# Deformable stage on TensorE: samples in column groups by tap, and one more tile of lead for the corner weights

## What is computed

```python
offset = conv2d(x, offset_w, offset_b)          # 3x3, 18 maps
mask = sigmoid(conv2d(x, mask_w, mask_b))       # 3x3, 9 maps
py = hs + ky + dy; px = ws + kx + dx            # one sampling point for each pixel and tap
val = gather(y0, x0) * w00 + gather(y0, x0 + 1) * w01 + gather(y0 + 1, x0) * w10 + gather(y0 + 1, x0 + 1) * w11
out = einsum('bkhwc,bkhw,ock->bohw', val, mask, w_r)     # 9 taps, 32 -> 32 channels
x = x + out                                     # x is normalised before the block
```

## Time and profile before

| | us |
|---|---|
| median of 3 runs | 2346.87 |
| lowest and highest | 2318.73, 2351.54 |
| the profiled execution | 2314.87 |
| its span in the profile | 2313.1 |
| attention, to | 850.17 |
| deformable stage, near part | 850.17 to 1573.10 |
| of this steady, from spread(2) to the last samples | 922.51 to 1564.84 |
| the rest | 1573.10 to 2313.10 |

### The profile page before, as it was taken

How to read it: one execution, slowest core, us unless ns; L and a number is a source line. 1 busy time by engine, 2 the same in 40 slices (tenths; PEclk the granted TensorE clock), 3 DMA queues, 4 the chain that set the end, 5 groups by cost and what they waited for, 6 DMA issues and landing times. The chain is left out here.

```text
span 2313.1 us, 46229 instructions
## 1 busy us (share of the span) xinstructions
PE 2045.3 (88%) x14981; PEld 1256.5 (54%) x14981; DVE 1281.6 (55%) x2688; ACT 1133.4 (49%) x3617; POOL 788.5 (34%) x743
## 2 busy tenths in 40 slices
PE   5699999999999963999999999995694999999999
PEld 3566666666666641232333333324682877777776
DVE  5178888888888871555555555555336222222222
ACT  2378888888888853555555555540121111111111
POOL 0178788787887841222222222210000110110110
PEclk9889999999999985898898998887777999999999
DMA  4300000000000015444444444415002112112110
GB/s 165 110 25 27 26 24 27 26 28 26 26 27 26 24 45 144 123 133 127 121 126 120 123 133 129 108 47 91 10 10 66 34 34 66 33 33 65 34 33 14
DMA packets 169883, 149.70 MB, mean 65 GB/s; under 512 B 60645, under 2 KB 159563, under 8 KB 169694
## 3 DMA queue, kind: packets, MB, share of 16 engines
q1 hardware_dynamic: 169774, 148.38, 24.2%
HBM read 83.68 MB, written 45.89 MB: 56 GB/s over the span
## 5 line engine op out<-in xcount | busy, mean ns | idle before, releaser
L412 ACT ACTIVATE at_probs<-at_sc,at_nmx 128x196 f32<-128x196 f32 x1152 | 473.7, 424 | 116.9 <-DVE at_nmx L358 114.8
L340 POOL TENSOR_TENSOR at_probs<-at_probs,at_rs 128x784 f32<-128x784 f32 x288 | 429.9, 1493 | 156.6 <-DVE at_rs L363 156.6
L447 PE MATMUL at_pt<-at_ident,at_probs 128*98 128x128 f32 x2304 | 312.7, 279 | 40.7 <-DVE at_pts L368 40.1
L358 DVE TENSOR_REDUCE at_nmx<-at_sc 128x4 f32<-128x784 f32 x288 | 277.7, 964 | 124.7 <-PE at_sc L436 124.7
L1237 ACT ACTIVATE dn_mix<-dn_mps 128x432 f32<-128x432 f32 x384 | 182.6, 527 | 297.3 <-PE dn_mps L1139 296.8
L447 PEld LDWEIGHTS at_pt<-at_ident,at_probs 128*98 128x98 f32 x2304 | 242.0, 129 | 142.2 <-POOL at_probs L340 78.6
L436 PE MATMUL at_sc<-at_kw,at_qw 32*128 32x196 f32 x2304 | 273.5, 357 | 12.0 <-POOL at_qw L329 8.0
L1330 DVE COPY dn_sampled<-dn_sps 128x432 f32<-128x432 f32 x192 | 116.7, 608 | 252.3 <-PE dn_sps L1150 251.4
L1139 PE MATMUL dn_mps<-dn_stack,dn_selw 42*128 42x432 f16 x768 | 199.0, 383 | 52.9 <-DMA dn_stack<-near_corners 47.4
L1323 DVE TENSOR_SCALAR dn_mix<-dn_mps 128x432 f32<-128x432 f32 x384 | 213.8, 598 | 44.4 <-PE dn_mps L1139 44.4
L2014 PE MATMUL fc_qps<-fc_wk,fc_xs 99*128 99x128 f32 x1728 | 207.9, 277 | 31.6 <-DMA fc_xs<-in_ones 31.6
(11 more groups left out here) (153 smaller groups left out, 2397.6 us busy)
## 6 DMA issues: line engine op xcount, KB each, us to landing
fc_xs<-fc_xp SPq DMA_DIRECT2D x144, 120.0 KB
dn_slab<-near_image SPq DMA_DIRECT2D x72, 200.0 KB, 3.7
at_vs<-attention_values SPq DMA_DIRECT2D x288, 49.0 KB
near_corners<-dn_split SPq DMA_DIRECT2D x24, 486.0 KB
dn_stack<-near_corners SPq DMA_DIRECT2D x24, 486.0 KB
dn_patch<-near_pixels SPq DMA_DIRECT2D x24, 384.0 KB
attention_values<-ap_vrow SPq DMA_DIRECT2D x21, 256.0 KB, 2.3
near_image<-dn_chunk SPq DMA_DIRECT2D x24, 200.0 KB, 1.9
```

The costliest lines, as they stand in the source:

```text
L340: nc.gpsimd.tensor_tensor(probs[s][p][:, :, :, :], probs[s][p][:, :, :, :], rs[s][:, 2 * p:2 * p + 2, :].unsqueeze(3).broadcast_to([P, 2, ...
L358: nc.vector.tensor_reduce(nmx[s][:, 2 * p:2 * p + 2, :], sc[p][:, :, 0:2 * NK].rearrange("p b (j k) -> p b j k", j=2), AX.X, ALU.max, nega ...
L412: nc.scalar.activation(probs[s][p][:, b, j, :], sc[p][:, b, NK * j:NK * j + NK], ACT.Exp, bias=nmx[s][:, 2 * p + b, j:j + 1], accum_out=su ...
L447: mm = nc.tensor.transpose(pt[b % 2][0:HK, o:o + P], probs[s][p][:, b % 2, j, HK * c:HK * c + HK], ident[:, :])
```

## The change

*Samples.* Taps 0 to 7 are now laid out by column group: tap 4u + g of batch b goes to columns 32g of the array, and to columns 96b + 48u of sps. Each batch has four matmuls of 2 x 48 = 96 columns, and tap 8 one of 48 in the batch's old place: 20 matmuls a step in place of 4. So sampled has four taps on its partitions, and one contraction matmul of 128 rows sums over four taps and 32 channels: contract is three calls of four matmuls, for each batch into its 32 columns, at k = 1 to 3. wd shrinks to six 128 x 32 blocks.

*Lead.* Maps, hats and corner weights run one tile further ahead: conv(t + 4), bias_maps(t + 3), prepare(t + 2) at k = 1 to 4, high(t + 2) at k = 6, with the calls ahead of the loops added to match, among them conv(3) ahead of spread(0). SyncE's list is reordered, with store_corners(t + 1) first.

*Maps.* The maps are stored by batch and tap, y, x and mask next to each other, and one transfer loads all three, each row three times. residual moves from k = 6 to 4, and stack has batch ahead of tap.

```diff
-        stack = [sb(f"stack{i}", [STACK, TAPS, B, 3 * DR, THIRD], F16) for i in range(2)]
+        stack = [sb(f"stack{i}", [STACK, B, TAPS, 3 * DR, THIRD], F16) for i in range(2)]
...
-                for a, to in enumerate((hat_y, off_x, mask)):
-                    sp.dma_start(to[:, :], map_d[j % 2, TAPS * a:TAPS * a + TAPS, :, :].rearrange("k b n -> (k b) n").unsqueeze(1).broadcast_to([TAPS * B, 3, DPX])
-                                 ).then_inc(rep_in, 16)
+                sp.dma_start(offs[:, :, :].rearrange("p a n -> p (a n)"),
+                             map_d[j % 2, :, :, :].rearrange("b (k a) n -> (b k) (a n)", a=3).unsqueeze(1).broadcast_to([B * TAPS, 3, 3 * DPX])).then_inc(rep_in, 16)
...
             load_slab(2)
+            load_maps(1)
             store_corners(0)
             load_stack(0)
-            load_maps(1)
             store_pixels(2)
             store_image(4)
             store_pixels(3)
+            store_maps(2)
+            load_slab(3)
+            load_maps(2)
+            store_image(5)
             for t in range(DTILES):
                 if t + 1 < DTILES:
+                    store_corners(t + 1)
                     load_patch(t + 1)
-                save(t)
-                if t + 2 < DTILES:
-                    store_maps(t + 2)
                 if t + 3 < DTILES:
-                    load_slab(t + 3)
+                    store_maps(t + 3)
+                if t + 4 < DTILES:
+                    load_slab(t + 4)
+                if t + 1 < DTILES:
+                    load_stack(t + 1)
                 if t + 4 < DTILES:
                     store_pixels(t + 4)
-                if t + 5 < DTILES:
-                    store_image(t + 5)
-                if t + 2 < DTILES:
-                    load_maps(t + 2)
-                if t + 1 < DTILES:
-                    store_corners(t + 1)
-                    load_stack(t + 1)
+                if t + 6 < DTILES:
+                    store_image(t + 6)
+                save(t)
+                if t + 3 < DTILES:
+                    load_maps(t + 3)
...
                 for b in range(B):
-                    mm = nc.tensor.matmul(sps[C * b:C * b + C, 0:COLS], patch[t % 2][:, k, C * b:C * b + C], mix[s % 2][b][:, :], start=True, stop=True)
+                    fours = mix[s % 2][b][:, 0:8 * PX].rearrange("p (u g n) -> p u g n", u=2, g=4)
+                    for g in range(4):
+                        nc.tensor.matmul(sps[C * g:C * g + C, 2 * PX * b:2 * PX * b + 2 * PX], patch[t % 2][:, k, C * b:C * b + C], fours[:, :, g, :], start=True, stop=True)
+                for b in range(B):
+                    mm = nc.tensor.matmul(sps[C * b:C * b + C, 8 * PX:COLS], patch[t % 2][:, k, C * b:C * b + C], mix[s % 2][b][:, 8 * PX:COLS], start=True, stop=True)
...
-                mm = nc.tensor.matmul(ops[:, 0:DPX], wd[:, k, :], sampled[t % 2][:, k, :, :].rearrange("p m i -> p (m i)"), start=(k == 0), stop=(k == TAPS - 1))
-                if k == TAPS - 1:
+                for b in range(B):
+                    w, n = (k, 2 * b + k) if k < 2 else (2 + b, 8)
+                    mm = nc.tensor.matmul(ops[C * b:C * b + C, 0:DPX], wd[:, w, :], sampled[t % 2][:, n, :, :].rearrange("p m i -> p (m i)"),
+                                          start=(k == 0), stop=(k == 2))
+                if k == 2:
...
             for kx in range(3):
                 conv(2, kx)
+            for kx in range(3):
+                conv(3, kx)
             spread(0)
...
-                    if t >= 1:
-                        for tap in range(2 * k - 2, 2 * k):
-                            if 0 <= tap < TAPS:
-                                contract(t - 1, tap)
-                    if t + 3 < DTILES and k >= 5:
-                        conv(t + 3, k - 5)
+                    if t >= 1 and 1 <= k < 4:
+                        contract(t - 1, k - 1)
+                    if t + 4 < DTILES and k >= 5:
+                        conv(t + 4, k - 5)
...
-                    if t + 2 < DTILES and k == 0:
-                        bias_maps(t + 2)
-                    if t + 1 < DTILES and k == 2:
-                        high(t + 1)
-                    if t + 2 < DTILES and k >= 4:
-                        prepare(t + 2, k - 4)
+                    if t + 3 < DTILES and k == 0:
+                        bias_maps(t + 3)
+                    if t + 2 < DTILES and 1 <= k < 5:
+                        prepare(t + 2, k - 1)
+                    if t + 2 < DTILES and k == 6:
+                        high(t + 2)
```

More of the change, by code:

```diff
@@ L869 @@
 THIRD = W // 3
-COLS = TAPS * DR * DBW
+PX = DR * DBW
+COLS = TAPS * PX
 PATCH = (DR + 4) * (DBW + 4)
@@ L953, in stage_deform_near @@
                            (wd[:, :, :], dcn), (ident[:, :], ident_d),
-                           *((stack[i][DATA:STACK, :, :, :, :].rearrange("p t b m i -> p (t b m i)"), bars) for i in range(2))))
+                           *((stack[i][DATA:STACK, :, :, :, :].rearrange("p b t m i -> p (b t m i)"), bars) for i in range(2))))
         mean, rstd = agg[:, 0:1], agg[:, 3:4]
@@ L961, in stage_deform_near @@
         patch = [sb(f"patch{i}", [PATCH, DSTEPS, P]) for i in range(2)]
-        hat_y = sb("hat_y", [NROWS, DPX])
-        off_x = sb("off_x", [NROWS, DPX])
-        mask = sb("mask", [NROWS, DPX])
+        offs = sb("offs", [NROWS, 3, DPX])
+        hat_y, off_x, mask = (offs[:, a, :] for a in range(3))
         hat_x = sb("hat_x", [NROWS, 3, DPX])
@@ L1036, in store_maps @@
                 for b in range(B):
-                    sp.dma_start(map_d[j % 2, :, b, :], maps[j % 2][C * b:C * b + 27, :, :].rearrange("p m i -> p (m i)")).then_inc(map_out, 16)
+                    sp.dma_start(map_d[j % 2, b, :, :], maps[j % 2][C * b:C * b + 27, :, :].rearrange("p m i -> p (m i)")).then_inc(map_out, 16)
             def load_maps(j):
@@ L1056, in load_stack @@
                     sp.wait_ge(mix_done, B * DSTEPS * (j - 1))
-                sp.dma_start(stack[j % 2][0:DATA, :, :, :, :].rearrange("p t b m i -> p (t b) (m i)"),
+                sp.dma_start(stack[j % 2][0:DATA, :, :, :, :].rearrange("p b t m i -> p (b t) (m i)"),
                              corner_d[j % 2, :, :].rearrange("(g r) (h n) -> (r h) g n", r=3, n=DPX)).then_inc(stack_in, 16)
@@ L1138, in spread @@
                             pe.wait_ge(mix_act, 2 * (s - 1) + b - 1)
-                    nc.tensor.matmul(mps[b][:, 0:COLS], selw[:, :], stack[t % 2][:, :, b, :, 4 * k:4 * k + 4], start=True, stop=True).then_inc(mix_done, 1)
+                    nc.tensor.matmul(mps[b][:, 0:COLS], selw[:, :], stack[t % 2][:, b, :, :, 4 * k:4 * k + 4], start=True, stop=True).then_inc(mix_done, 1)
             def sample(s):
@@ L1202, in distance_y @@
             def distance_y(j):
-                act.wait_ge(rep_in, 48 * (j + 1))
-                rows = hat_y[:, :].rearrange("p (r n) -> p r n", r=DR)
+                act.wait_ge(rep_in, 16 * (j + 1))
+                rows = hat_y.rearrange("p (r n) -> p r n", r=DR)
                 for c in range(3):
@@ L1255, in _ @@
             high(0)
+            bias_maps(2)
             for part in range(4):
                 prepare(1, part)
+            high(1)
             for b in (2, 3):
@@ L1342, in _ @@
             normalise(3)
+            normalise(4)
             keep_rows(2)
-            normalise(4)
+            normalise(5)
             keep_rows(3)
@@ L1347, in _ @@
             largest(1)
+            largest(2)
             for b in range(2):
@@ L1357, in _ @@
                         keep_rows(t + 4)
-                    if k == 1 and t + 5 < DTILES:
-                        normalise(t + 5)
-                    if k == 2 and t + 2 < DTILES:
-                        largest(t + 2)
+                    if k == 1 and t + 6 < DTILES:
+                        normalise(t + 6)
+                    if k == 2 and t + 3 < DTILES:
+                        largest(t + 3)
                     keep(s)
-                    if k == 6 and t >= 1:
+                    if k == 4 and t >= 1:
                         residual(t - 1)
@@ L1376, in host_l1d @@
 def host_l1d(ow, ob, mw, mb, dw):
-    w3 = np.stack([ow[0::2], ow[1::2], mw]).reshape(27, C, 3, 3)
+    w3 = np.stack([ow[0::2], ow[1::2], mw], 1).reshape(27, C, 3, 3)
     convw = np.zeros((3, C, 3, C), np.float32)
@@ L1380, in host_l1d @@
     bias = np.zeros((B, C), np.float32)
-    bias[:, 0:27] = np.stack([ob[0::2], ob[1::2], mb]).reshape(27)
+    bias[:, 0:27] = np.stack([ob[0::2], ob[1::2], mb], 1).reshape(27)
     caps = np.zeros((B, C), np.float32)
-    caps[:, 0:18] = 2
+    caps[:, 0:27:3] = 2
+    caps[:, 1:27:3] = 2
     taps = dw.reshape(C, C, TAPS)
-    wd = np.zeros((B, C, TAPS, B, C), np.float32)
-    for b in range(B):
-        wd[b, :, :, b, :] = taps.transpose(1, 2, 0)
+    wd = np.zeros((4, C, 2 + B, C), np.float32)
+    for g in range(4):
+        for u in range(2):
+            wd[g, :, u, :] = taps[:, :, 4 * u + g].T
```

(1 more changed line is left out.)

26 lines of the change are left out of this document (13 added, 13 removed).

## The result

| | before | after |
|---|---|---|
| median of 4 runs, us | 2336.07 | 2118.67 |
| lowest and highest | 2318.73, 2351.54 | 2103.08, 2127.27 |
| profiled execution | 2314.87 | 2127.27 |
| attention, up to | 850.17 | 845.18 |
| deformable stage, near part | 722.9 | 516.2 |

The ratio is 0.9064, with a 95% interval of 0.897 to 0.9158: faster by 9.4%. A second set of four runs of the changed kernel gave 2139.59 us, ratio 0.9122 [0.9006, 0.9239]. Between the two profiled executions the stage gave 206.7 us and the attention 5.0; the rest took 24.1 more. None of the changed lines is in that rest.

What follows compares the result with a forecast made beforehand. TensorE was taken as the bound, slowed by the late corner-weight stack and the low clock behind it. Steady stretch -94, start-up +7, end -4 made -91 us off the 2346.87 median: 2256 us, range 2165 to 2330.

Steps and rivals of the forecast that it cites:

- The count of pairs: Near-tap deformable stage, steady stretch: 9512 pairs of weight load and pass on TensorE, 7640 of them in the samples.
- the row of the convolution: Profile row used to price contract: one group of four matmuls costs 0.67 us, so 2.0 us a tile instead of 6.7.
- the sum of 22.9: TensorE's parts of an old tile at 2.4 GHz: spread, sample, contract, convolution and transposes, 22.9 us of the tile's 26.9.
- Sample in column groups: Samples, 40 pairs a step instead of 8: array time stays 0.87 us, but delivery at 57 ns a pair sets the pace.
- a burst of 10 ns: Lower bound on a pair's price: a queued burst of eight pairs starts within 0.08 us, 10 ns a pair.
- the nearest row: L1722 of the Fourier stage, a long fp32 chain with 32 columns moving, 57 ns a pair, taken as the samples' price.
- the start-up: Before the first sample: conv(3) now stands ahead of spread(0), costing 7 us more, bounds 0 and 15.
- the array is the limit: Rival, chance 0.24: array time, not delivery, limits the near-tap stage; tile 19.7 us, stretch 461 us, kernel 2169 us.
- The 1.5 us a tile: Array rival's addition to its 18.2 us tile, where a residual or the distances on VectorE and ScalarE fall into a step.
- The low end of the range: 2165 us for the whole kernel, the array rival's case taken whole.
- The tail: Contraction behind the last tile: 18 passes of 6.07 us become some 2.2, 3.9 us less at the end.
- The claim on the median: Whole kernel: the 91 us reckoned on the profiled execution come off the median shown, 2346.87, giving 2256 us.

Runs made afterwards that it cites:

- lead_only: New order with the extra tile of lead and the one map load, samples and contraction as before, against the kernel before: 2220.71 us, ratio 0.9556.
- the chains: Changed kernel plus an added stage of fp32 matmul chains that wait for nothing, in several runs, varying column groups, weight spacing and length: 9 to 57 ns a pair.
- more_pairs: Changed kernel with each 96-column sample matmul cut into two of 48, 72 pairs a sample: 2293.40 us, ratio 0.9783 to the kernel before.

## Why the prediction was wrong

**What held.** The bound was named rightly: TensorE, with the late stack and the clock behind it. The count of pairs was exact (9512). A group of four taps of contract takes 0.67 us, as the row of the convolution said. The stack is hidden, the clock is 1.00, and no transfer that was moved is late. lead_only shows this half at -4.4%, with a tile of 22.3 us against the sum of 22.9.

**The step that failed** is in *Sample in column groups*, the price of a pair of weight load and pass: "Something that doesn't follow the array's clock delivers a pair every 57 ns. I take this". The price was bounded from below by a burst of 10 ns and from above by 68, and L1722 was taken as "the nearest row". That row was near in its column counts and far in what sets its price. It loads weights that lie 32 elements apart into one column group; the chains show 57 ns for this and 9 for four groups in turn with weights side by side. The samples are of the second kind: the earlier trace rows came nearer than the earlier trace rows, though its 10 ns were read off rounded lengths, and the eight starts lie 14 ns apart in the trace. With the pair at the array's own time the stretch takes 435 us in place of 548: 113 us. I took off 91 us; the two profiled executions differ by 187.6, which is 91, these 113, 3 for the start-up, 5 for the attention, less 24 for the rest.

**The argument behind it** was that a burst comes from a filled queue and a chain at the rate of delivery. A rate of delivery does exist, but it is 28 to 31 ns a pair in the chains and 40 in more_pairs, and it comes in blocks of 128 pairs. It was never the 57 ns of L1722. At 45.8 ns a pair the kernel after hardly touches it; more_pairs does. "It is also the densest chain of the whole trace, so nothing contradicts it" was a lack of evidence taken for evidence. The figure of about 62 ns that the Trainium skill has (TensorE: Matmul & The Clock Gate, Back-to-back issue gap), quoted beside it, isn't seen in any chain with weights side by side.

**The rival "the array is the limit"** is what happened, at 0.24. Its tile of 18.2 us from PE's own parts was exact: 23.9 of them are 435 us. The 1.5 us a tile that it added for crowding on VectorE and ScalarE were wrong: both still waited for PE for 74.6 and 100.0 us. With 435 us in place of its 461 its time, 26 us less than 2169, is 2143. The low end of the range was hung on this rival and was too high by as much.

**Smaller terms.** The start-up was to cost 7 us and costs 3.7. The slab of tile 3 was issued 61.5 us into the stage in place of 65.4, and was used 4.95 us later in place of 5.9; but the first sample came 4.0 us behind the convolution and not 2.0, with the spreads of two steps and four transposes between them. The tail gave 3.5 us of the 4. For waits I took 4 us, and PE stood for 5.9 in the stretch.

**The claim on the median.** I took 91 us off the median shown, 2346.87. The median of four is 2336.07, so 11 us of the miss lie in the base, and the medians differ by 217.4 where the profiled executions do by 187.6.

## What to carry to other kernels

The price of a small matmul is not a constant to be read off the row that looks alike. Ask of that row whether its weights are contiguous and whether the next matmul goes to another column group: between the four cases the price went from 9 to 57 ns. Then compare two sums for each stretch, the array's columns and the number of pairs times the price of delivery, 30 ns in the chains and 40 beside this stage's transfers; while the first is well above the second, cutting matmuls up is nearly free (1.6 ns a pair here), and near the second PE runs dry and loses its clock as well. And where two limits lie on top of each other, here a late transfer and the array, the halves of a change can be worth -4.4% and +0.9% alone and -9.4% together.

## What the runs showed of the hardware

- Pairs of fp32 weight load and pass, 32 columns of weights and 32 moving, at 2.4 GHz: 32 ns in one column group, 9 ns with four groups in turn (13 ns at 1.2 GHz). The Trainium skill (TensorE: Matmul & The Clock Gate, Wait — 56ns, not 53.3ns?) says that starts never come closer than about 25 ns. Across column groups the measurement decides against that: 165 starts in 1.46 us.
- Weights 32 elements apart make a pair 57 ns in one group, and 18 ns with four in turn. The 57 ns are the same at 1.2 and 2.4 GHz, the 18 ns at a granted clock of 0.79 and 0.50.
- Straight-line code comes to PE in blocks of 256 instructions, 3.47 to 4.02 us apart with the transfer engines idle, 3.47 to 4.30 with them at 0.7 and above, and one in 5.1 us in the mean in more_pairs (DMA share 0.44).
- Two fp16 matmuls of 42 rows at partitions 0 and 64, each over all 128 columns, run side by side: four take 0.47 us in place of 0.83.
